# Attention block: the last half's small transfers issued from ScalarE's queue, and a second set of PSUM banks for the output projection

## The chip, the cores and the metric

The kernel runs on one NeuronCore of a Trainium2 chip. The metric is the device time in microseconds (us). It was run three times: 1845.27 us is the median, 1840.76 the lowest and 1845.5 the highest.

## What is computed

The reference is one block with attention and a feed-forward part beside each other. The input is 4 batches of 1024 tokens of width 256. There are 16 heads of 64, taken as 8 pairs. The feed-forward weights and activations are rounded to FP4 in blocks of 16.

```python
xn = _layernorm(x, axis=-1)
x = x + attn(xn, Wq, Wkv, Wout, bout) + ffn(xn, w_gate, w_up, w_down)
# attn: q, k, v = split_heads(xn @ Wq, xn @ Wkv); q, k = _rope(q), _rope(k)
#       sim = einsum('bhid,bhjd->bhij', q, k) * SCALE; p = softmax(sim)
#       out = einsum('bhij,bhjd->bhid', p, v) -> (b, n, 1024);  out @ Wout + bout
```

## The kernel before

The kernel has four parts, written out for each engine: preparation, feed-forward, attention and output. The order of an engine's instructions is the order of the code, and semaphores order the engines among each other. Every DMA is issued by SyncE (sp) from its one queue, in which SyncE also waits: a wait there holds back all transfers behind it.

**Attention** runs in 32 steps s (4 batches times 8 pairs of heads), each of two halves of 512 queries. Halves are numbered 0 to 63. A half's unnormalised output grows in the PSUM bank `o_ps` (bank 7) and is copied to `o_raw` by ScalarE (`copy_o`). Its row sums come from a product with ones in `misc_ps` (bank 2) and are copied to `sum_rows` by ScalarE (`copy_sums`, L1256). Then six transfers and two small operations follow. `store_sums` (L1318) writes the sums to HBM and reads them back in compact form, 8 values to a partition. VectorE takes the reciprocal (`invert`, L1119). `spread_inverse` (L1326) writes that to HBM and reads it back spread over the rows, once for each head. GpSimd multiplies (`normalise`, L1171), and `store_o` (L1336) writes the half to `o_scratch`.

**The output** runs over 8 groups n of 4 tiles of 128 tokens. `load_o(n)` reads 2 MB of `o_scratch` into `o_in[n % 2]`. ScalarE copies each tile's high part (`high`, L1513), VectorE subtracts to get the low part (`split`, L1521), and TensorE multiplies by Wout, 24 matrix multiplications to a tile (`multiply`, L1546). VectorE adds the rest, that is the input, the bias and the feed-forward result (`sums`, L1533). SyncE loads that rest (`load_rest`, L1491) and stores the result (`store`, L1497). All groups write tile t into bank 3 + t, so that tile t of group n waits until `sums` has read tile t of group n - 1 (L1542). `o_hl` and `o_in` have two buffers: `high(n)` waits for the multiplications of group n - 2 and `load_o(n)` for `split(n - 2)`.

**The order around the change.** TensorE multiplies group 0, then the sums of half 63, then groups 1 to 7. ScalarE goes: copy_o(63), high(1), copy_sums(63), high(2), high(3) and so on. VectorE goes: sums(0) and split(1) interleaved, invert(63), then split(2), sums(1), split(3), sums(2), and so on to sums(7). SyncE's end of attention is L1416 to L1428, and then its loop over n from 4 is load_o(n), load_rest(n), store(n - 2). In this order load_o(4) stands behind the whole chain of half 63.

PSUM has 8 banks. In attention banks 0, 1, 5 and 6 hold scores, 3 and 4 the estimates of the maxima, 2 projections and sums, 7 the output.

Of the kernel before, what the change touches and what calls it, by code (L numbers as in the profile page):

```python
# [27 lines left out]
P = 128  # L28
# [807 lines left out]
def attention_part(nc, zones, banks, sem, io, kept, output):  # L836
# [48 lines left out]
    scored, exp_done, pv_done, added = kept["scored"], sem("exp_done"), kept["pv_done"], kept["added"]  # L885
    o_copied, sums_copied = sem("o_copied"), sem("sums_copied")
    sum_stored, compact_in, inv_done, inv_stored = sem("sum_stored"), sem("compact_in"), sem("inv_done"), sem("inv_stored")
    inv_spread = [sem(f"inv_spread{i}") for i in range(2)]
    normed = sem("normed")
    o_stored, rest_stored = kept["o_stored"], kept["rest_stored"]  # L890
    bout_in, rest_in, biased, rest_added = sem("bout_in"), [sem(f"rest_in{i}") for i in range(2)], sem("biased"), sem("rest_added")
# [168 lines left out]
    def vector(dve):  # L1060
# [54 lines left out]
        def invert(half):  # L1115

            dve.wait_ge(compact_in, 16 * (half + 1))
            b = half % 2
            nc.vector.reciprocal(inv_compact[:, b, :, :], compact[:, b, :, :]).then_inc(inv_done, 1)  # L1119
# [42 lines left out]
    def gpsimd(pool):  # L1162
        def normalise(half):

            b = half % 2
            pool.wait_ge(inv_spread[b], 32 * (half // 2 + 1))
            pool.wait_ge(o_copied, half + 1)
# [51 lines left out]
    def scalar(act):  # L1219
# [30 lines left out]
        def copy_sums(half):  # L1250
# [5 lines left out]
            nc.scalar.activation(sum_rows[half % 2][:, :], misc_ps[:, 0:SUMS], ACT.Copy).then_inc(sums_copied, 1)  # L1256

        for chunk in (K1, Q0, Q1):
            high(act, 0, chunk)
        ffn_over(act)  # L1260
        for s in range(-1, STEPS + 1):
            for r in range(ROUNDS):
# [21 lines left out]
                if r == 2 and scoring(s - 1):  # L1284
                    copy_sums(2 * (s - 1) + 1)
                if r == 6 and scoring(s):
                    copy_sums(2 * s)
# [21 lines left out]
    def sync(sp):  # L1309
# [110 lines left out]
        store_o(2 * last)  # L1420
        store_sums(2 * last + 1)
        output["load_rest"](sp, 2)
        output["store"](sp, 0)
        output["load_o"](sp, 3)
        spread_inverse(2 * last + 1)
        store_o(2 * last + 1)
        output["load_rest"](sp, 3)
# [29 lines left out]
def output_part(nc, zones, banks, sem, io, kept):  # L1457
# [6 lines left out]
    o_in = [bound("o_in0", [P, PAIRS, GCOL], F32), free("o_in1", [P, PAIRS, GCOL], F32)]  # L1464
    ps = [banks[:, 3 + t, 0:D] for t in range(GRP)]
    GROUPS = TILES // GRP
# [6 lines left out]
    def load_o(sp, n):  # L1473

        b, u = divmod(n, 2)
        if n >= 2:

            sp.wait_ge(o_low, GRP * (n - 1))
        sp.wait_ge(o_stored[u], 16 * HALVES_OF * (b + 1))
        sp.dma_start(o_in[u][:, :, :], io["o_scratch"][b * PAIRS:(b + 1) * PAIRS, :, u * GCOL:(u + 1) * GCOL]  # L1480
                     .rearrange("s p n -> p s n")).then_inc(o_loaded[u], 16)
# [42 lines left out]
    def sums(dve, n, tiles=range(GRP)):  # L1524
# [6 lines left out]
        for t in tiles:  # L1531
            dve.wait_ge(mult_done, n * GRP + t + 1)
            nc.vector.tensor_tensor(out[u][:, t, :], ps[t], rest[u][:, t, :], ALU.add).then_inc(out_ready, 1)  # L1533

    def multiply(pe, n):
# [3 lines left out]
        for t in range(GRP):  # L1539
            pe.wait_ge(o_low, n * GRP + t + 1)  # L1540
            if n:
                pe.wait_ge(out_ready, (n - 1) * GRP + t + 1)  # L1542
            k = 0
            for os, ws in PARTS:
                for c in range(PAIRS):
                    ins = nc.tensor.matmul(ps[t], o_hl[n % 2][:, os, c, t * P:(t + 1) * P],  # L1546
                                           wo[:, ws, c * D:(c + 1) * D], start=k == 0, stop=k == 3 * PAIRS - 1)
# [34 lines left out]
def build(nc, io):  # L1582
    with ExitStack() as whole:
# [18 lines left out]
        for name in ("x_low", "silu_done", "h_done", "h_high", "down_done", "res_ready", "wo_low", "misc_done", "turn_done", "scored",  # L1602
                     "pv_done", "added"):
            kept[name] = sem(name)
# [107 lines left out]
```

## Time and profile before

| | us |
|---|---|
| median of three runs | 1845.27 |
| lowest and highest | 1840.76 and 1845.5 |
| the profiled execution | 1844.23 |
| its span | 1842.5 |
| TensorE busy | 1760.6 (96%) |
| VectorE busy | 1448.3 (79%) |
| ScalarE busy | 1064.8 (58%) |
| GpSimd busy | 1396.5 (76%) |

The profile is of one execution. Its span runs from the first to the last instruction, and 1.7 us lie around it. PE is TensorE's multiplication, PEld its loading of weights, DVE VectorE, ACT ScalarE, POOL GpSimd, and SPq the queue of SyncE. A time such as 1761.18 is in us from the start of the span. A bracket behind an instruction says how long its engine stood idle before it and what ended that.

### The profile page before, as it was taken

The numbers are of one execution on the slowest core, as the hardware profiler recorded it, in microseconds if no ns is written. First come the engines' busy times: TensorE is split into PE (matmuls) and PEld (weight loads), VectorE is DVE, ScalarE is ACT, GpSimd is POOL, SyncE is SP. The second block draws the span as 40 slices with busy tenths as digits, with TensorE's granted clock in tenths as the row PEclk, the third lists the DMA queues.
The fourth block names the chain that finished last, engine by engine and source line by source line (L and its number), as shares of the span: only waits on it lengthen the run. The fifth ranks groups of instructions, "written<-read, shape, count | busy, mean of one in ns | idle before, by whom it ended". The sixth has DMA issues, their size and how long they took to land.

```text
span 1842.5 us, 29200 instructions
## 1 busy us (share of the span) xinstructions
PE 1760.6 (96%) x10596; PEld 1088.6 (59%) x10596; DVE 1448.3 (79%) x2034; ACT 1064.8 (58%) x1334; POOL 1396.5 (76%) x688
## 2 busy tenths in 40 slices
PE   6979999968999999999999999999999999999889
PEld 4768999944555555555555555555555555554589
DVE  7978999978788878887888788778877887884353
ACT  4642333315666666666666666666666666667531
POOL 3863544415898989999989899999899999999800
PEclk9999999988999999999999999999999999999899
DMA  8651221121233342332224322333433233322574
GB/s 290 238 201 43 73 105 38 47 72 46 73 86 89 93 139 85 88 89 86 85 90 127 104 85 88 87 86 86 127 94 100 84 90 85 87 73 77 186 264 154
DMA packets 164591, 195.11 MB, mean 106 GB/s; under 512 B 48352, under 2 KB 112736, under 8 KB 164192
## 3 DMA queue, kind: packets, MB, share of 16 engines
q1 hardware_dynamic: 164448, 193.25, 33.5%
q8 instruction: 84, 1.38, 0.3%
q14 instruction: 59, 0.48, 0.1%
HBM read 133.69 MB, written 59.51 MB: 105 GB/s over the span
## 4 chain that ended last, share of the span: by engine, by line
PE 61%; DVE 21%; issue 6%; POOL 2%; DMA 2%; ACT 1%; SPq 0%; DVEq 0%; POOLq 0%; ACTq 0%
PE banks L1025 19%; PE banks L1003 15%; PE banks L945 11%; PE banks L979 8%; PE banks L1546 3%; DVE half_max L1069 3%; PE banks L1008 3%; PE banks L1034 2%; DVE h_scales L110 2%; DVE banks L1103 2%; POOL acc L1189 2%; DMA o_in<-o_scratch 2%; DVE f_y L131 2%; DVE f_amax L109 2%; DVE f_y L134 2%
## 5 line engine op out<-in xcount | busy, mean ns | idle before, releaser
L1189 POOL TENSOR_TENSOR acc<-acc,prob 128x1024 f32<-128x1024 f32 x384 | 919.0, 2393 | 78.9 <-ACT prob L1228 46.7
L1069 DVE TENSOR_REDUCE half_max<-banks 128x2 f32<-128x1024 f32 x512 | 627.2, 1226 | 217.9 <-PE banks L979 215.5
L1228 ACT ACTIVATE prob<-banks 128x1024 f32<-128x1024 f32 x512 | 509.8, 1023 | 397.5 <-PE banks L1008 389.8
L1025 PE MATMUL banks<-prob,v 128*64 128x512 f32 x2048 | 495.7, 605 | 0.0
L1240 ACT ACTIVATE banks<-max_all 128x1024 f32<-128x1024 f32 x256 | 263.4, 1029 | 15.3 <-DVE half_max L1069 3.4
L1025 PEld LDWEIGHTS banks<-prob,v 128*64 128x64 f32 x2048 | 124.4, 136 | 227.6 <-issue 189.9
L979 PE MATMUL banks<-k_hi,q_hi 64*128 64x512 f32 x1024 | 232.1, 451 | 17.8 <-DVE half_max L1069 16.2
L979 PEld LDWEIGHTS banks<-k_hi,q_hi 64*128 64x128 f32 x1024 | 96.5, 186 | 233.5 <-issue 125.9
L1189 POOL TENSOR_TENSOR acc<-prob,prob 128x1024 f32<-128x1024 f32 x64 | 153.8, 2402 | 91.9 <-ACT prob L1228 91.9
L945 PE MATMUL banks<-xT,wqk 128*128 128x512 f32 x768 | 217.3, 419 | 2.1 <-DVE k_lo L1112 2.1
L1003 PE MATMUL banks<-q_hi,k_hi 64*128 64x512 f32 x1024 | 204.3, 395 | 8.7 <-ACT prob L1228 8.7
L1003 PE MATMUL banks<-q_hi,k_lo 64*128 64x512 f32 x1024 | 202.5, 391 | 0.0
L1003 PE MATMUL banks<-q_lo,k_hi 64*128 64x512 f32 x1024 | 202.0, 390 | 0.0
L945 PEld LDWEIGHTS banks<-xT,wqk 128*128 128x128 f32 x768 | 137.4, 192 | 61.3 <-issue 33.5
L135 POOL TENSOR_TENSOR f_y<-f_y,f_m 128x704 f32<-128x704 f32 x32 | 54.7, 1710 | 130.0 <-DVE f_y L134 130.0
L732 PE MATMUL banks<-wgT,xqT 128*128 128x352 f32 x768 | 133.9, 329 | 6.3 <-DVE h L583 4.5
L732 PEld LDWEIGHTS banks<-wgT,xqT 128*128 128x128 f32 x768 | 123.7, 190 | 8.7 <-DVE h L583 6.5
L1092 DVE TENSOR_TENSOR crossed<-banks,rope 128x512 f32<-128x512 f32 x128 | 88.5, 691 | 41.2 <-PE banks L945 39.6
L1003 PEld LDWEIGHTS banks<-q_hi,k_hi 64*128 64x128 f32 x1024 | 97.1, 186 | 26.5 <-ACT prob L1228 12.8
L1003 PEld LDWEIGHTS banks<-q_hi,k_lo 64*128 64x128 f32 x1024 | 96.8, 185 | 22.7
L1003 PEld LDWEIGHTS banks<-q_lo,k_hi 64*128 64x128 f32 x1024 | 96.8, 185 | 22.1
L1546 PE MATMUL banks<-wo,o_hl 128*128 128x256 f32 x768 | 95.8, 288 | 6.9 <-DVE out L1533 6.7
(121 smaller groups left out, 2138.5 us busy)
## 6 DMA issues: line engine op xcount, KB each, us to landing
max_all<-max_scratch SPq DMA_DIRECT2D x64, 512.0 KB, 4.1
v_scratch<-v_out SPq DMA_DIRECT2D x32, 512.0 KB, 2.6
wqk<-wp_scratch SPq DMA_DIRECT2D x32, 512.0 KB, 3.8
v<-v_scratch SPq DMA_DIRECT2D x32, 512.0 KB, 5.9
inv_rows<-inv_scratch SPq DMA_DIRECT2D x128, 128.0 KB, 3.3
o_scratch<-o_norm SPq DMA_DIRECT2D x64, 256.0 KB, 2.2
o_in<-o_scratch SPq DMA_DIRECT2D x8, 2048.0 KB, 11.2
xn_scratch<-p_xT SPq DMA_DIRECT2D x32, 256.0 KB, 2.9
```

The costliest lines, as they stand in the source:

```text
L732: ins = nc.tensor.matmul(ps[:, a, 0:FH], xqT[:, t, xs, c, :], wgT[:, ws, c, w, a * FH:(a + 1) * FH], start=k == 0, stop=k == 3 * DC - 1)
L945: ins = nc.tensor.matmul(bank(s, chunk), wqk[s % 2][:, ws, c, col:col + P], xT[:, 4 * half:4 * half + 4, xs, c, :], start=k == 0, stop=k = ...
L979: ins = nc.tensor.matmul(guess_bank(s, i)[:, head, :], q_hi[s % 3][rows, t * P:(t + 1) * P], k_hi[s % 3][rows, part * 512:(part + 1) * 512 ...
L1003: ins = nc.tensor.matmul(s_ps[n % 2][:, head, :], left[rows, keys], right[rows, queries], start=k == 0 and not has_seed, stop=k == 2 and h ...
L1008: ins = nc.tensor.matmul(s_ps[n % 2][:, head, :], first_row[rows, :], max_all[half][rows, head, :], start=False, stop=True)
L1025: ins = nc.tensor.matmul(o_ps[head * DH:(head + 1) * DH, :], v[s % 2][:, kt, at:at + DH], prob[n % SLOTS][:, head, :], start=kt == 0, stop ...
L1069: nc.vector.tensor_reduce(half_max[:, half % 2, :, t % GRP, part], guess_bank(s, i), axis=AX.X, op=ALU.max, negate=True).then_inc(half_max ...
L1092: nc.vector.tensor_tensor(crossed[a][:, :], bank(s, chunk), rope[:, 1, pos], ALU.mult).then_inc(crossed_done, 1)
L1189: nc.gpsimd.tensor_tensor(acc[b][:, :, :], first, prob[n % SLOTS][:, :, :], ALU.add).then_inc(added, 1)
L1228: nc.scalar.activation(prob[n % SLOTS][:, :, :], s_ps[n % 2][:, :, :], ACT.Exp).then_inc(exp_done, 1)
L1240: nc.scalar.activation(s_ps[n % 2][:, :, :], max_all[u // QT][:, :, :].bitcast(F32), ACT.Copy).then_inc(seeded, 1)
L1546: ins = nc.tensor.matmul(ps[t], o_hl[n % 2][:, os, c, t * P:(t + 1) * P], wo[:, ws, c * D:(c + 1) * D], start=k == 0, stop=k == 3 * PAIRS - 1)
```

## The change

The six transfers of half 63 move from SyncE's queue to ScalarE's. `finish_last_half` is placed in ScalarE's order right behind copy_sums(63), ahead of high(2), with its own semaphores (`end_sums`, `end_compact`, `end_inv`, `end_spread`, `end_o`), for which invert, normalise and load_o(7) wait. They are gone from SyncE's order. Groups of odd number use banks 0, 1, 2 and 7 in place of 3 to 6; tile t of group n waits for the sums of group n - 2, and group 1 for the copies out of banks 2 and 7.

```diff
@@ -883,10 +883,11 @@
     max_turn = sem("max_turn")
     max_stored, max_in = [sem(f"max_stored{i}") for i in range(2)], [sem(f"max_in{i}") for i in range(2)]
     scored, exp_done, pv_done, added = kept["scored"], sem("exp_done"), kept["pv_done"], kept["added"]
-    o_copied, sums_copied = sem("o_copied"), sem("sums_copied")
+    o_copied, sums_copied = kept["o_copied"], kept["sums_copied"]
     sum_stored, compact_in, inv_done, inv_stored = sem("sum_stored"), sem("compact_in"), sem("inv_done"), sem("inv_stored")
     inv_spread = [sem(f"inv_spread{i}") for i in range(2)]
     normed = sem("normed")
+    end_sums, end_compact, end_inv, end_spread = sem("end_sums"), sem("end_compact"), sem("end_inv"), sem("end_spread")
     o_stored, rest_stored = kept["o_stored"], kept["rest_stored"]
     bout_in, rest_in, biased, rest_added = sem("bout_in"), [sem(f"rest_in{i}") for i in range(2)], sem("biased"), sem("rest_added")
 
...
@@ -1114,7 +1115,10 @@
 
         def invert(half):
 
-            dve.wait_ge(compact_in, 16 * (half + 1))
+            if half == HALVES - 1:
+                dve.wait_ge(end_compact, 16)
+            else:
+                dve.wait_ge(compact_in, 16 * (half + 1))
             b = half % 2
             nc.vector.reciprocal(inv_compact[:, b, :, :], compact[:, b, :, :]).then_inc(inv_done, 1)
 
...
@@ -1163,7 +1167,10 @@
         def normalise(half):
 
             b = half % 2
-            pool.wait_ge(inv_spread[b], 32 * (half // 2 + 1))
+            if half == HALVES - 1:
+                pool.wait_ge(end_spread, 32)
+            else:
+                pool.wait_ge(inv_spread[b], 32 * (half // 2 + 1))
             pool.wait_ge(o_copied, half + 1)
             if half >= 2:
 
...
@@ -1254,6 +1261,23 @@
 
                 act.wait_ge(sum_stored, 16 * (half - 1))
             nc.scalar.activation(sum_rows[half % 2][:, :], misc_ps[:, 0:SUMS], ACT.Copy).then_inc(sums_copied, 1)
+
+        def finish_last_half():
+
+            half = HALVES - 1
+            b = half % 2
+            act.wait_ge(sums_copied, half + 1)
+            act.dma_start(io["sum_scratch"][b].rearrange("h (k c) -> (h k) c", k=2), sum_rows[b][0:P:QROWS, :]).then_inc(end_sums, 16)
+            act.wait_ge(end_sums, 16)
+            act.dma_start(compact[:, b, :, :], io["sum_scratch"][b].rearrange("h (p f) -> p h f", f=GRP)).then_inc(end_compact, 16)
+            act.wait_ge(inv_done, half + 1)
+            act.dma_start(io["inv_scratch"][b].rearrange("h (p f) -> p h f", f=GRP), inv_compact[:, b, :, :]).then_inc(end_inv, 16)
+            act.wait_ge(end_inv, 16)
+            for head in range(2):
+                act.dma_start(inv_rows[b][head * DH:(head + 1) * DH, :],
+                              io["inv_scratch"][b, head].partition_broadcast(DH)).then_inc(end_spread, 16)
+            act.wait_ge(normed, half + 1)
+            act.dma_start(io["o_scratch"][half // 2, :, b * GCOL:(b + 1) * GCOL], o_norm[b][:, :]).then_inc(kept["end_o"], 16)
 
         for chunk in (K1, Q0, Q1):
             high(act, 0, chunk)
...
@@ -1283,6 +1307,8 @@
                     copy_o(2 * s)
                 if r == 2 and scoring(s - 1):
                     copy_sums(2 * (s - 1) + 1)
+                if r == 2 and s == STEPS:
+                    finish_last_half()
                 if r == 6 and scoring(s):
                     copy_sums(2 * s)
 
...
@@ -1418,12 +1444,9 @@
         spread_inverse(2 * last)
         output["load_o"](sp, 2)
         store_o(2 * last)
-        store_sums(2 * last + 1)
         output["load_rest"](sp, 2)
         output["store"](sp, 0)
         output["load_o"](sp, 3)
-        spread_inverse(2 * last + 1)
-        store_o(2 * last + 1)
         output["load_rest"](sp, 3)
         output["store"](sp, 1)
 
...
@@ -1462,7 +1485,7 @@
     rest = [left(f"rest{i}", [P, GRP, D], F32) for i in range(2)]
     out = [left(f"out{i}", [P, GRP, D], F32) for i in range(2)]
     o_in = [bound("o_in0", [P, PAIRS, GCOL], F32), free("o_in1", [P, PAIRS, GCOL], F32)]
-    ps = [banks[:, 3 + t, 0:D] for t in range(GRP)]
+    ps = [[banks[:, k, 0:D] for k in group] for group in ((3, 4, 5, 6), (0, 1, 2, 7))]
     GROUPS = TILES // GRP
     HALVES_OF = PAIRS
 
...
@@ -1476,7 +1499,11 @@
         if n >= 2:
 
             sp.wait_ge(o_low, GRP * (n - 1))
-        sp.wait_ge(o_stored[u], 16 * HALVES_OF * (b + 1))
+        if n == GROUPS - 1:
+            sp.wait_ge(o_stored[u], 16 * (HALVES_OF * (b + 1) - 1))
+            sp.wait_ge(kept["end_o"], 16)
+        else:
+            sp.wait_ge(o_stored[u], 16 * HALVES_OF * (b + 1))
         sp.dma_start(o_in[u][:, :, :], io["o_scratch"][b * PAIRS:(b + 1) * PAIRS, :, u * GCOL:(u + 1) * GCOL]
                      .rearrange("s p n -> p s n")).then_inc(o_loaded[u], 16)
 
...
@@ -1530,7 +1557,7 @@
             dve.wait_ge(stored[u], 16 * (n // 2))
         for t in tiles:
             dve.wait_ge(mult_done, n * GRP + t + 1)
-            nc.vector.tensor_tensor(out[u][:, t, :], ps[t], rest[u][:, t, :], ALU.add).then_inc(out_ready, 1)
+            nc.vector.tensor_tensor(out[u][:, t, :], ps[u][t], rest[u][:, t, :], ALU.add).then_inc(out_ready, 1)
 
     def multiply(pe, n):
 
...
@@ -1538,12 +1565,16 @@
             pe.wait_ge(kept["wo_low"], 2)
         for t in range(GRP):
             pe.wait_ge(o_low, n * GRP + t + 1)
-            if n:
-                pe.wait_ge(out_ready, (n - 1) * GRP + t + 1)
+            if n >= 2:
+                pe.wait_ge(out_ready, (n - 2) * GRP + t + 1)
+            elif n == 1 and t == 2:
+                pe.wait_ge(kept["sums_copied"], HALVES)
+            elif n == 1 and t == 3:
+                pe.wait_ge(kept["o_copied"], HALVES)
             k = 0
             for os, ws in PARTS:
                 for c in range(PAIRS):
-                    ins = nc.tensor.matmul(ps[t], o_hl[n % 2][:, os, c, t * P:(t + 1) * P],
+                    ins = nc.tensor.matmul(ps[n % 2][t], o_hl[n % 2][:, os, c, t * P:(t + 1) * P],
                                            wo[:, ws, c * D:(c + 1) * D], start=k == 0, stop=k == 3 * PAIRS - 1)
                     k += 1
             ins.then_inc(mult_done, 1)
```

## Rows read from the trace of the kernel before

**Rows 1.** The page, part 1: busy us (share of the span) xinstructions

```profile
PE 1760.6 (96%) x10596; PEld 1088.6 (59%) x10596; DVE 1448.3 (79%) x2034; ACT 1064.8 (58%) x1334; POOL 1396.5 (76%) x688
```

**Rows 2.** Timeline of PE: start us, us, engine, line, operation, out<-in, xcount [idle before]

```profile
1747.72 11.77 PE L1546 MATMUL banks<-wo,o_hl 128*128 128x256 f32 x96
1761.18 23.63 PE L1546 MATMUL banks<-wo,o_hl 128*128 128x256 f32 x192 [1.69 <-DVE out L1533]
1789.86 48.72 PE L1546 MATMUL banks<-wo,o_hl 128*128 128x256 f32 x384 [5.05 <-DVE out L1533]
```

**Rows 3.** Stretches: from:to us, length, busy of engines, PEclk, DMA share, GB/s

```profile
1788.00:1789.00 1.00, 0.00 (x0) 0.00 (x0) 1.00 (x2) 0.00 (x0) 0.00 (x0) 0.76 1.05 387
1795.00:1796.00 1.00, 1.00 (x9) 1.00 (x9) 1.00 (x2) 0.68 (x1) 0.00 (x0) 0.83 1.06 380
```

**Rows 4.** Waits, 1740 to the end: us in total, times, longest

```profile
PE banks L1546 <- DVE out L1533: 6.7, 2, 5.0
```

**Rows 5.** Timelines of ACT and DVE, 1748 to 1792

```profile
1748.80 0.36 ACT L1256 ACTIVATE sum_rows<-banks 128x256 f32<-128x256 f32 x1
1753.47 3.90 ACT L1513 ACTIVATE o_hl<-o_in 128x1024 fp32r<-128x1024 f32 x4 [4.30 <-DMA o_in<-o_scratch]
1783.65 3.90 ACT L1513 ACTIVATE o_hl<-o_in 128x1024 fp32r<-128x1024 f32 x4 [13.98 <-DMA o_in<-o_scratch]
1791.78 3.90 ACT L1513 ACTIVATE o_hl<-o_in 128x1024 fp32r<-128x1024 f32 x4 [4.23 <-DMA o_in<-o_scratch]
...
1784.74 4.63 DVE L1521 TENSOR_TENSOR o_hl<-o_in,o_hl 128x1024 fp32r<-128x1024 f32 x4 [10.84 <-ACT o_hl L1513]
1789.30 1.41 DVE L1533 TENSOR_TENSOR out<-banks,rest 128x256 f32<-128x256 f32 x4
```

**Rows 6.** Timeline of SyncE's queue, 1744 to 1780 (some rows left out)

```profile
1744.25 0.53 SPq L1480 DMA_DIRECT2D o_in<-o_scratch  x1
...
1749.19 0.52 SPq L1322 DMA_DIRECT2D sum_scratch<-sum_rows  x1
1754.32 0.35 SPq L1324 DMA_DIRECT2D compact<-sum_scratch  x1
...
1755.84 0.45 SPq L1480 DMA_DIRECT2D o_in<-o_scratch  x1
1756.33 1.78 SPq L1330 DMA_DIRECT2D inv_scratch<-inv_compact  x1
1765.94 1.10 SPq L1333 DMA_DIRECT2D inv_rows<-inv_scratch  x2
1771.53 0.34 SPq L1340 DMA_DIRECT2D o_scratch<-o_norm  x1
...
1773.06 0.46 SPq L1480 DMA_DIRECT2D o_in<-o_scratch  x1
...
1776.99 3.12 SPq L1480 DMA_DIRECT2D o_in<-o_scratch  x1
```

**Rows 7.** Timelines of SyncE's queue and of POOL: the chain's steps at quieter places

```profile
1611.88 0.53 SPq L1322 DMA_DIRECT2D sum_scratch<-sum_rows  x1
1613.52 0.36 SPq L1324 DMA_DIRECT2D compact<-sum_scratch  x1
...
1740.85 0.45 SPq L1330 DMA_DIRECT2D inv_scratch<-inv_compact  x1
1743.05 1.11 SPq L1333 DMA_DIRECT2D inv_rows<-inv_scratch  x2
...
1746.63 1.83 POOL L1171 TENSOR_TENSOR o_norm<-o_raw,inv_rows 128x512 f32<-128x512 f32 x1 [1.75 <-DMA inv_rows<-inv_scratch]
1770.12 1.38 POOL L1171 TENSOR_TENSOR o_norm<-o_raw,inv_rows 128x512 f32<-128x512 f32 x1 [21.66 <-DMA inv_rows<-inv_scratch]
```

**Rows 8.** Stretches, columns as in rows 3: one with the DMA engines full

```profile
1760.00:1763.00 3.00, 1.81 (x15) 1.85 (x16) 2.03 (x5) 0.00 (x0) 0.00 (x0) 1.00 1.05 404
```

**Rows 9.** Tile compact, its 64 loads: us from issue to landing

```profile
DMA to landing us min/median/max: 1.7/1.7/3.2
```

More of the change, by code:

```diff
@@ L1602, in build @@
         for name in ("x_low", "silu_done", "h_done", "h_high", "down_done", "res_ready", "wo_low", "misc_done", "turn_done", "scored",
-                     "pv_done", "added"):
+                     "pv_done", "added", "end_o", "o_copied", "sums_copied"):
             kept[name] = sem(name)
```

## Prediction

> **What bounds the kernel now.** I read the page first, then only the end of the span, since the diff leaves the instruction order of everything before the last step alone. The busy lines [rows 1] say that TensorE is the bound overall (96%), so the change can only give back idle time of TensorE in the output stage, and it can only cost by making new idle time there. The timeline of TensorE in that stage [rows 2] is to be read for its holes. From group 1 on it runs 96, 192 and 384 multiplications with two holes: 1759.49 (1747.72 + 11.77) to 1761.18, and 1784.81 to 1789.86. That is 1.69 and 5.05 us. A group lasts 11.8 us (23.63 / 2). The last four took 48.72 us where four times 11.77 is 47.08, so 1.64 us more. The stretches of the clock [rows 3] show why: TensorE stopped at 1784.81, the granted clock was down to its lower level (1.2 GHz) by 1789 (mean 0.76 over 1788 to 1789, so it fell about 3.9 us after the stop), and it was back at 2.4 GHz only in the slice 1795 to 1796. After the hole of 1.69 us it did not fall. All that can be won is thus 1.69 + 5.05 + 1.64 = 8.4 us, or 0.45% of the time.
>
> The waits [rows 4] name VectorE's addition L1533 as what ended both holes. The reason lies in the order on VectorE: split(2) and only then sums(1), split(4) and only then sums(3), while the next group needs the bank that sums frees. For the second hole there is more behind it: ScalarE's high(4) started at 1783.65, the moment o_in(4) landed [rows 5], and that load had been issued only at 1773.06, because SyncE's queue stood from 1756.33 to 1771.53 in the chain of the last half (inverse to scratch, spread, normalise, store) [rows 6].
>
> **The change part by part.**
>
> **The second set of banks.** Group n no longer waits for sums(n - 1), but for sums(n - 2), which is over long before. Banks 0, 1, 2 and 7 are free for group 1: the sums are copied out at 1749.16 [rows 5] while tile 2 of group 1 comes at about 1747.72 + 5.9 = 1753.6; o_ps was copied earlier still. No instruction is added but waits that are already met, so the cost is nothing; if the copy came after 1753.6, each us late would be a us of hole. The gain by itself: a group may start when its first split is done. From the start h of high, the split begins 1.1 us later (1783.65 to 1784.74), takes 1.16 us (4.63 / 4), and TensorE follows 0.2 us behind (VectorE's addition ended at about 1789.65, TensorE began at 1789.86): h + 2.5. For group 4 that is 1786.15 where it was 1789.86. With nothing else changed group 2 would start at 1759.5 and the hole before group 4 would be about 1786.15 - 1783.1 = 3.0 us. By then the clock was still at 2.4 GHz in the hole of before. So this part alone is worth 8.4 - 3.0 = 5.4 us.
>
> **The chain off SyncE's queue.** SyncE issued the six transfers of the last half (sum_scratch, compact, inv_scratch, two inv_rows, o_scratch) between its own. Without them load_o(3) goes when split(1) is done, at 1751.9 instead of 1755.84, and load_rest(3), store(1) and load_o(4) are bound by VectorE alone (sums(1), and split(2) for load_o(4)). The last load needs the new end_o, which is over some 30 us before: nothing.
>
> **The chain on ScalarE's queue.** This adds the wait that decides. finish_last_half stands ahead of high(2), and in it ScalarE waits in turn for sum_scratch, for VectorE's reciprocal, for inv_scratch and for GpSimd's normalise. Queued behind it are the four copies high(2) for which split(2) on VectorE waits, behind those sums(1), and so group 2 on TensorE, load_rest(3), store(1) and load_o(4) on SyncE. Before, high(2) ran at 1753.47, as soon as o_in(2) was there. Now it starts at h, when the chain has ended. Undisturbed, by its steps [rows 7]: sum_scratch to the issue of compact 1.64 (1611.88 to 1613.52); compact, reciprocal and issue of inv_scratch 2.01 (1754.32 to 1756.33); inv_scratch 2.20 (1740.85 to 1743.05); the two inv_rows to the start of the normalisation 3.58 (1743.05 to 1746.63); the normalisation and the issue behind it 1.41 (1770.12 to 1771.53); that issue itself 0.34. Sum 11.2, so h is 1749.16 + 11.2 = 1760.4 at the earliest. The time TensorE stands still before group 2 is h + 2.5 - 1759.5, so at least 3.4 us where it was 1.69.
>
> But the chain does not run undisturbed. SyncE's load_o(2) is under way from 1744.25, and behind it now stand load_rest(2) and store(0) (0.5 MB each, about 1749) and load_o(3) (2 MB, at 1751.9): some 5.5 MB with store_o(62), which at the 404 GB/s of a full stretch [rows 8] keep the DMA engines full from about 1746 to 1759.6. No row of this case shows a transfer of a second queue beside a full one. The bounds are these. Below: no delay, h = 1760.4. Above: each waits for all that was issued before it, as on the one queue of before, where sum_scratch took 5.13 us (1749.19 to 1754.32) and inv_scratch 9.61 us (1756.33 to 1765.94). Then compact lands with load_o(3) at about 1760.4, and with 0.3 + 2.20 + 3.58 + 1.41 + 0.34 behind it h is 1768.2; at the very worst the chain keeps its whole length of before, from 1749.16 to 1771.87, and h is 1771.9. I take a value nearer to the lower end: queues that take turns. At 404 GB/s over 16 engines a piece of 2 KB takes 81 ns; compact and inv_scratch are cut in 256 pieces of 16 bytes, 16 to an engine, and if each stands behind one of 2 KB that is 1.3 us for either. sum_scratch has four pieces and the two inv_rows fall behind the full stretch: about 0.1. That is an estimate from these rows: h = 1760.4 + 2.7 = 1763.1.
>
> The Trainium skill, on its page DMA: Bandwidth & Descriptors (Queues, rings and completion order), says that each DMA engine takes turns between the queues that have work for it, a packet at a time, and the section Issuing engines are not separate DMA queues that all of them still run on the same 16 engines. No run here shows either yet. The first speaks for an h between 1760.4 and 1763.1, the second against an undisturbed chain.
>
> **The sum.** After group 2 starts, nothing else is late. load_o(4) is issued after split(2), sums(1), load_rest(3) and store(1), at about h + 8.3; group 4 is due at h + 2.5 + 23.6 = h + 26.1. Even if the load took the 14.8 us that load_o(5) took beside another (1776.99 to 1791.78) it gives a start of h + 8.3 + 14.8 + 2.5 = h + 25.6, just in time; with the 10.6 us of load_o(4) itself there are 4.7 us to spare. The loads behind it keep the rhythm that they had, and there TensorE had no hole. So groups 2 to 7 take 23.63 + 47.08 = 70.7 us, and TensorE ends at h + 2.5 + 70.7, plus the clock. Before it was 1789.86 + 48.72 = 1838.58; what lies behind (one addition, one store) stays. The difference is h - 1765.4, plus 1.64 for the clock where the hole outlasts the 3.9 us after which it fell before, which it does from h = 1760.9 on. With h = 1763.1 the hole is 6.1 us and the difference -2.3 + 1.64 = -0.7 us: the span goes from 1842.5 to 1841.8, the profiled execution from 1844.23 to 1843.5. The median of the three runs (1845.27) lies 1.0 above the profiled one, and I forecast from it: 1844.6.
>
> **The rivals.**
>
> **The chain as quick as undisturbed.** The small transfers pass between the large ones at no price: h = 1760.4, hole 3.4 us, no fall of the clock: -5.0, so 1840.3. For it: they are tiny, and their median landing over 64 halves is short (compact 1.7 us [rows 9]). Against it: every step of the chain but the last lies in the full stretch.
>
> **The small ones wait for the large ones: slower.** A queue of its own does not help, because the pieces of SyncE's loads are already handed to the same engines, or because both queues' pieces are made out by one unit; SyncE's own issue of inv_scratch took 1.78 us right behind load_o(3) against 0.45 for the half before, and load_o(5) 3.12 against 0.46. The place is compact and inv_scratch; the price is h = 1768.2, +2.8 + 1.64 = +4.4, so 1849.7, and up to h = 1771.9, +8.1, so 1853.4. It decides from h = 1763.8 on, where the gain of the banks is used up (h - 1765.4 + 1.64 = 0). Against it: load_o(3) goes 4 us earlier than before, so that it is through when inv_rows are due.
>
> **A second hole remains.** The hole before group 4 stays, because load_o(4) takes longer than any did: 1 us of hole for each us over 15. That speaks only for a little more than the forecast, 1846 to 1848.
>
> **The banks alone count.** If ScalarE's chain hid wholly behind group 1, that is h at most 1757.0, the whole 8.4 us would come back: 1836.9. It would need a chain of 7.8 us, 3.4 less than its undisturbed steps; I see no row for it.
>
> **How the numbers follow.** Forecast (h from 1761.2 to 1766, 1842.7 to 1847.5) 0.5; undisturbed chain (1838.5 to 1842) 0.22; small behind large (1848 to 1853.4) 0.2; second hole 0.06; all comes back 0.02. A measurement of this kernel can tell about 0.3% from no change, that is 5.5 us: under 1839.7 or over 1850.8. Faster takes under half of the undisturbed case and the last: 0.1. Slower takes about half of the third: 0.1. The rest, 0.8, is within. The range of 1839.5 to 1850 leaves out the upper half of the third case and a tail of the second, some 0.15 to 0.2.
>
> **What would show it.** In the profile after: TensorE's timeline of L1546 with one hole, of about 6 us, before group 2, ended by VectorE's split L1521 and no longer by L1533, the low clock behind it, and no hole before group 4; high(2) on ScalarE at 1763 where it was 1753; GpSimd's last normalisation near 1761.5 instead of 1770.12; load_o(4) at about 1771. The landings of compact and inv_scratch under ScalarE's queue settle the rivals: 1.7 and 2.2 us, 3.0 and 3.5, or over 5. It is wrong if the hole before group 2 is under 3 or over 9 us, if a hole shows later, or if anything ahead of 1740 differs.

## The result and the profile after

The change makes the kernel slower, by 0.3%: the median is 1849.85 us (1847.46 to 1850.47, 7 runs) against 1844.05 for the kernel before (1840.76 to 1845.5, 7 runs). The ratio is 1.003, with a 95% interval of 1.0021 to 1.0039. The profiled execution took 1848.66 us with a span of 1846.9, where before it was 1844.23 and 1842.5. Two executions among the experiments' (2860.54 us of chain_only, 3419.98 of late_chain) were in a far slower state; the ratios leave them out, and the medians of these two kernels hardly move by them (0.2 us at most).

The timeline of TensorE after, beside [rows 2]:

```profile
1748.39 11.77 PE L1577 MATMUL banks<-wo,o_hl 128*128 128x256 f32 x96
1771.55 71.39 PE L1577 MATMUL banks<-wo,o_hl 128*128 128x256 f32 x576 [11.39 <-DVE o_hl L1548]
```

Two holes, of 1.69 and 5.05 us, have become one of 11.39. Groups 2 to 7 then run without another, and what ends the hole is no longer the addition but the split. It is the start of everything for group 2 that is late. Of the 4.4 us between the two spans, 0.7 lie ahead of group 1 (1748.39 against 1747.72), where the code is the same; over all the profiled executions of this document group 1 starts between 1746.74 and 1749.29, a spread that no edit here explains. The timelines of ScalarE and its queue, and of VectorE and GpSimd, show what came first (columns as in [rows 2]):

```profile
1748.95 0.36 ACT L1263 ACTIVATE sum_rows<-banks 128x256 f32<-128x256 f32 x1
1749.34 1.08 ACTq L1270 DMA_DIRECT2D sum_scratch<-sum_rows  x1
1754.85 0.39 ACTq L1272 DMA_DIRECT2D compact<-sum_scratch  x1
1761.65 0.37 ACTq L1274 DMA_DIRECT2D inv_scratch<-inv_compact  x1
1763.78 1.14 ACTq L1277 DMA_DIRECT2D inv_rows<-inv_scratch  x2
1768.73 0.34 ACTq L1280 DMA_DIRECT2D o_scratch<-o_norm  x1
1769.18 7.69 ACT L1540 ACTIVATE o_hl<-o_in 128x1024 fp32r<-128x1024 f32 x8 [19.87 <-POOL o_norm L1178]
...
1761.41 0.20 DVE L1123 RECIPROCAL inv_compact<-compact 128x8 f32<-128x8 f32 x1 [9.45 <-DMA compact<-sum_scratch]
1770.27 4.63 DVE L1548 TENSOR_TENSOR o_hl<-o_in,o_hl 128x1024 fp32r<-128x1024 f32 x4 [8.65 <-ACT o_hl L1540]
...
1767.44 1.26 POOL L1178 TENSOR_TENSOR o_norm<-o_raw,inv_rows 128x512 f32<-128x512 f32 x1 [18.83 <-DMA inv_rows<-inv_scratch]
```

ScalarE issues sum_scratch at 1749.34 and comes to high(2) at 1769.18, where it was 1753.47 [rows 5]. From one to the other are 19.84 us. On SyncE's queue in the kernel before, the chain took 22.7 us (1749.19 to 1771.87), but there nothing of group 2 stood behind it. The steps compare with the quiet ones of [rows 7] like this: sum_scratch 5.51 us against 1.64, compact with the reciprocal 6.80 against 2.01, inv_scratch 2.13 against 2.20, inv_rows 3.66 against 3.58. So two steps are long, the two that ran while SyncE's loads were under way, and they are 8.7 us too long together (3.9 for sum_scratch, 4.8 for compact). What SyncE had issued by then:

```profile
1744.55 0.53 SPq L1507 DMA_DIRECT2D o_in<-o_scratch  x1
1748.63 0.34 SPq L1366 DMA_DIRECT2D o_scratch<-o_norm  x1
1749.08 0.40 SPq L1518 DMA_DIRECT2D rest<-rest_scratch  x1
1749.53 0.73 SPq L1524 DMA_DIRECT2D out<-out  x1
1751.99 0.36 SPq L1507 DMA_DIRECT2D o_in<-o_scratch  x1
1776.25 0.36 SPq L1518 DMA_DIRECT2D rest<-rest_scratch  x1
```

The last two rows also show the second cost: behind load_o(3) SyncE issues nothing for 24 us, since load_rest(3) waits for sums(1), and sums(1) stands behind split(2) on VectorE. The profile's DMA answer for two stretches of the changed kernel counts each queue's packets (q1 is SyncE's queue, q10 ScalarE's; packets, MB, share of 16 engines, over 100% where the recorded times of packets overlap). A piece is one such packet of data: compact has 256 of 16 bytes, load_o(3) 1024 of 2 KB. First the stretch that follows the issue of compact, then a microsecond later on:

```profile
q1 hardware_dynamic: 944, 1.31, 105.4%
```

```profile
q1 hardware_dynamic: 186, 0.38, 98.4%
q10 hardware_dynamic: 178, 0.00, 10.1%
```

From 1754.85 to 1758.2 no packet of ScalarE's queue moves at all, though compact has been issued and waits for no semaphore. Its first piece moves at 1758.5, 3.6 us after the issue, and its last at 1760.9. From 1759 to 1760 the two queues move one for one. For inv_scratch, which is cut the same way and ran when only the end of load_o(3) was left, the first piece moved 0.9 us after the issue, and all of them took 0.7 us. So compact landed 4.4 us later than inv_scratch (6.5 us against 2.1), and 2.7 of these are more wait in front of its first piece and 1.7 are taking turns. For sum_scratch the wait was longer: its first piece moved at 1754.0, 4.7 us after its issue.

### The profile page after: what moved, and what is told of

The parts are those of the page before. It is cut to its first block, busy times and chain, and to the rows that moved or that the text cites. A ratio compares the mean times of both kernels' runs of the same rounds, so it can differ in the third digit from the quotient of the medians.

```text
span 1846.9 us, 29198 instructions
## 1 busy us (share of the span) xinstructions
PE 1761.7 (95%) x10596; PEld 1090.2 (59%) x10596; DVE 1446.6 (78%) x2034; ACT 1064.7 (58%) x1334; POOL 1395.4 (76%) x688
## 4 chain that ended last, share of the span: by engine, by line
PE 64%; DVE 20%; issue 6%; POOL 3%; ACT 0%; POOLq 0%; DVEq 0%; ACTq 0%
PE banks L1026 19%; PE banks L1004 16%; PE banks L946 11%; PE banks L980 9%; PE banks L1577 4%; PE banks L1009 3%; DVE half_max L1070 3%; POOL acc L1196 2%; PE banks L1035 2%; DVE h_scales L110 2%; DVE f_y L131 2%; DVE f_amax L109 2%; DVE f_y L134 2%; DVE h L583 1%; DVE banks L1104 1%
```

## The experiments

Changes in time are against the kernel before as run beside each experiment. Its median was 1842.97 us (14 runs) beside banks_only, chain_only, hold_load and late_chain, and 1842.85 (15 runs) beside hold_spread, large_pieces, act_split and pool_chain. Beside the changed kernel itself it was 1844.05, so kernels are compared by their distance from the kernel before: +5.8 us for the changed one. By the intervals of the ratios such a distance is good to 2 or 3 us either way. The diffs show the main lines of each edit; "..." stands for lines left out.

**The two parts by themselves.** `banks_only` is the kernel before with the second set of banks:

```diff
-    ps = [banks[:, 3 + t, 0:D] for t in range(GRP)]
+    ps = [[banks[:, k, 0:D] for k in group] for group in ((3, 4, 5, 6), (0, 1, 2, 7))]
...
-            if n:
-                pe.wait_ge(out_ready, (n - 1) * GRP + t + 1)
+            if n >= 2:
+                pe.wait_ge(out_ready, (n - 2) * GRP + t + 1)
...
```

> The change without its transfers: the second set of banks alone, the chain of half 63 on SyncE's queue as before. Theory (the banks give, the move of the chain takes): group 2 follows group 1 without a hole, high(2) stays near 1753.5, and the hole before group 4 shrinks from 5.05 to about 3.0 us, without the low clock behind it; 5.4 us less than before, about 1838.7. Rival (the loss sits in the new banks, or they give nothing since the loads are what is late): 1844 to 1850, the hole before group 4 still 5 us or more.

Measured: 1839.29 us, ratio 0.9978 (0.9969 to 0.9987), 3.7 us less. TensorE's timeline:

```profile
1748.97 34.81 PE L1550 MATMUL banks<-wo,o_hl 128*128 128x256 f32 x288
1785.91 47.82 PE L1550 MATMUL banks<-wo,o_hl 128*128 128x256 f32 x384 [2.12 <-DVE o_hl L1521]
```

Groups 1 to 3 run in one piece, and before group 4 a hole of 2.12 us is left, ended by the split as the arithmetic wanted. But what was expected of the clock did not come. The row of this kernel for 1787 to 1788 (columns as in [rows 3]) shows TensorE at work with the lower clock:

```profile
1787.00:1788.00 1.00, 1.00 (x7) 1.00 (x6) 1.00 (x1) 0.44 (x1) 0.00 (x0) 0.50 1.07 412
```

The mean granted clock is 0.92 from 1786 to 1787, 0.50 from 1787 to 1790 and 0.88 from 1790 to 1791: it fell near 1786.8, 0.9 us after TensorE had started again. The last four groups took 47.82 us, 1.6 more than four of the 11.56 us that a group takes where nothing stops (late_chain below). The banks are a gain all the same.

`chain_only` is the changed kernel with the old banks and the old wait.

```diff
-    ... for group in ((3, 4, 5, 6), (0, 1, 2, 7))]
+    ... for group in ((3, 4, 5, 6), (3, 4, 5, 6))]
```

> The change without its banks: the chain of half 63 issued by ScalarE, one set of banks. Theory: compact lands over 6 us after its issue as in the changed kernel, high(2) starts at about 1769, and TensorE now waits besides until sums(1) has read the banks, which comes after the whole of split(2), so group 2 starts some 3.5 us later still: about 1853.3. Rival (the move by itself costs little, the two parts only get in each other's way): about 1844 to 1847.

Measured: 1852.26 us, ratio 1.0046 (1.0032 to 1.006), 9.3 us more; compact landed after 6.5 us again, high(2) began at 1768.46, and group 2 in this row:

```profile
1774.66 71.81 PE L1573 MATMUL banks<-wo,o_hl 128*128 128x256 f32 x576 [14.09 <-DVE out L1560]
```

The hole of 14.09 us is ended by the addition again. So the move of the chain costs 9.3 us and the banks give 3.7; the sum of the two, 5.6, is close to the 5.8 of the change, though with 2 or 3 us of doubt in each it is a weak test. With the chain in place the banks bring 9.3 - 5.8 = 3.5 us.

**What makes the chain long.** `hold_load` lets SyncE issue load_o(3) only when inv_scratch has landed:

```diff
+        sp.wait_ge(kept["end_inv"], 16)
         output["load_o"](sp, 3)
```

> The changed kernel with one wait more: SyncE issues load_o(3), the 2 MB load that runs beside the chain, only once inv_scratch has landed. Theory (the small transfers on ScalarE's queue wait for the pieces that SyncE has issued before them): compact lands about 2.5 us after its issue in place of 6.5, inv_scratch keeps its 2.1, high(2) starts near 1765 in place of 1769.2, and the time is 4.1 us under that of the changed kernel, about 1845.8. Rival (transfers issued by ScalarE, or reading back what has just been written, are slow by themselves): compact still 6 us or more, 1849.9 or above since load_o(3) comes later.

Measured: 1850.24 us, ratio 1.0036 (1.0023 to 1.005), +7.3 us and no gain over the changed kernel. The queue of ScalarE shows both why the theory stands and why my number fell:

```profile
1754.10 0.39 ACTq L1272 DMA_DIRECT2D compact<-sum_scratch  x1
1756.89 0.37 ACTq L1274 DMA_DIRECT2D inv_scratch<-inv_compact  x1
1758.50 1.15 ACTq L1277 DMA_DIRECT2D inv_rows<-inv_scratch  x2
1768.30 0.34 ACTq L1280 DMA_DIRECT2D o_scratch<-o_norm  x1
```

compact took 2.79 us to the next issue in place of 6.80. But load_o(3) went at 1758.50, in the same moment as inv_rows, and now inv_rows were slow: they landed 6.5 and 7.9 us after their issue. I had let the load start one step too early, and the wait had only moved to it. `hold_spread` waits for both inv_rows instead:

```diff
+        sp.wait_ge(kept["end_spread"], 32)
         output["load_o"](sp, 3)
```

> As hold_load, but SyncE issues load_o(3) only once both inv_rows have landed, so that no large load is issued while the chain runs. In hold_load the reciprocal came 4.75 us earlier than in the changed kernel, and the two inv_rows, issued at the same moment as load_o(3), took 6.5 and 7.9 us in place of 3. Theory (a small transfer pays for what is issued before or with it, on either queue): inv_rows 3 us again, high(2) at about 1764 in place of 1769, load_o(3) still in time, 4.5 us under the changed kernel, about 1845. Rival (the chain is held by something else, such as ScalarE's own issuing): high(2) still near 1768, about 1850.

Measured: 1844.52 us, ratio 1.0011 (1.0001 to 1.002), +1.7 us, which is 4.1 less than the changed kernel's +5.8. The landings are 3.0 (compact) and 3.2 us (inv_rows). In this execution everything is 0.7 us later than in the one of the changed kernel, and high(2) starts 16.3 us after the copy of the sums where it was 20.2:

```profile
1749.61 0.36 ACT L1263 ACTIVATE sum_rows<-banks 128x256 f32<-128x256 f32 x1
1765.91 3.90 ACT L1541 ACTIVATE o_hl<-o_in 128x1024 fp32r<-128x1024 f32 x4 [15.94 <-POOL o_norm L1178]
...
1768.28 71.80 PE L1578 MATMUL banks<-wo,o_hl 128*128 128x256 f32 x576 [7.22 <-DVE o_hl L1549]
```

So it is load_o(3) beside the chain that made it 3.9 us longer, and not ScalarE's issuing. The 16.3 us still hold 5.6 for sum_scratch, which runs beside load_o(2). No run took load_o(2) away, so that these 5.6 us, too, come from loads under way is argued: from 1.64 us at a quiet place [rows 7], 5.13 on SyncE's queue before and from the packets.

**What a small transfer waits for.** `large_pieces` is the changed kernel in which load_o(3) has 8 pieces to an engine in place of 64. Group 3 is computed from other parts of o_scratch.

```diff
+        if n == 3:
...
+            sp.dma_start(o_in[u][:, :, :].rearrange("p s n -> p (s n)"),
+                         io["o_scratch"][at:at + 4].rearrange("s p n -> (s p n)").rearrange("(q m) -> q m", q=P)) ...
```

> The changed kernel, in which load_o(3) reads the same 2 MB in 128 pieces of 16 KB in place of 1024 pieces of 2 KB; they are other parts of o_scratch, so group 3 is computed from wrong data. It tells apart what compact waits for. In the changed kernel its first piece moved 3.6 us after the issue, behind 984 pieces of SyncE's queue (62 to an engine) or 1.4 MB. If a fixed number of pieces stands ahead: all 8 large pieces of each engine come first, compact lands only when load_o(3) is through, 7.5 us or more after its issue. If a fixed number of bytes: 6.5 us as before. If the making of the pieces is what it waits for: 3 us or less, since there are 8 times fewer, and high(2) starts near 1765.

Measured: compact landed after 9.0 us, and the single time was 1849.84. The number is near that of the first theory, but the packets say something else. From 1754.64 (the issue of compact) to 1758, and from 1758.5 to 1761:

```profile
q1 hardware_dynamic: 865, 1.47, 115.0%
```

```profile
q1 hardware_dynamic: 67, 1.10, 102.4%
q10 hardware_dynamic: 65, 0.00, 1.5%
```

In front of the first piece lies the same wait as in the changed kernel, some 3.5 us and 1.4 MB or a little more; and then the queues take turns by the piece, 65 pieces of 16 bytes against 67 of 16 KB. None of the three answers that I had written down is right by itself. The length has two parts, a wait in front and a turn for each piece, and only the second grew with the pieces of load_o(3).

Two runs ask what the wait in front is. Both start from hold_load, where inv_rows and load_o(3) are issued together while nothing else moves. `hold_large` gives load_o(3) its 128 large pieces as above, and `hold_small` 1024 pieces of 256 bytes:

```diff
+            sp.dma_start(o_in[u][:, :, 0:64], io["o_scratch"][b * PAIRS:(b + 1) * PAIRS, :, u * GCOL:u * GCOL + 64]
...
```

> As hold_load (load_o(3) issued by SyncE at the same moment as inv_rows by ScalarE, nothing else under way), but load_o(3) reads its 2 MB in 128 pieces of 16 KB in place of 1024 of 2 KB, from other parts of o_scratch, so group 3 is computed from wrong data. In hold_load the first piece of inv_rows moved 3.7 us after the issue. If what holds a small transfer back is the making of the pieces of the transfer issued before it, the first piece of inv_rows moves within 1.5 us of the issue here; if it is the bytes under way, after 3 us or more as there. Then the two queues take turns piece by piece, 8 to an engine against pieces of 0.65 us, so that inv_rows lands 6 us or more after its issue in either case.

> As hold_load, but load_o(3) reads only 64 of the 512 columns, 256 bytes a piece: still 1024 pieces, but 0.25 MB; the rest of o_in keeps what load_o(1) left, so group 3 is computed from wrong data. If the making of the pieces holds inv_rows back, its first piece moves 3 us or more after the issue as in hold_load, and it lands after 5 us or more; if the bytes under way do, within 1.5 us, and it lands after about 3.

Measured: single times of 1850.14 us (`hold_large`) and 1847.81 (`hold_small`), where the kernel before took 1842.89 beside them; and, by stretches of the DMA answer, the following. `hold_load`, 1758.5 to 1762.2 (nothing of q10), then 1762.2 to 1763:

```profile
q1 hardware_dynamic: 229, 0.47, 63.9%
```

```profile
q1 hardware_dynamic: 124, 0.25, 82.9%
q10 hardware_dynamic: 28, 0.06, 18.4%
```

`hold_large`, 1758.4 to 1763 (nothing of q10), then 1763 to 1765:

```profile
q1 hardware_dynamic: 63, 1.03, 70.5%
```

```profile
q1 hardware_dynamic: 47, 0.77, 92.5%
q10 hardware_dynamic: 31, 0.06, 8.2%
```

`hold_small`, 1761.2 to 1762.9 (nothing of q10):

```profile
q1 hardware_dynamic: 204, 0.05, 12.9%
```

What the same two transfers do with nothing beside them, `hold_spread` shows: issued at 1760.4, nothing until 1762.0, and from 1762 to 1764 all of both:

```profile
q10 hardware_dynamic: 160, 0.26, 49.2%
```

So with no load at all the first piece of inv_rows moves 1.6 us after the issue. Beside the 2 KB pieces it was 3.9 us (1762.4), beside the 16 KB pieces 5.2 (1763.6), and beside the 256 byte pieces 2.2 (1763.4). What the load adds is 2.3, 3.6 and 0.6 us. The landings were 6.5 and 7.9, 8.9 and 9.3, 4.0 and 4.1 us, against 3.2 alone. Both runs speak for the bytes under way, though `hold_small` missed the numbers written down for that (1.5 us to the first piece, 3 to the landing). The fewest pieces made the longest wait, and 1024 small ones added 0.6 us, so the making of the pieces is at most a small part of it. It goes with the bytes that are under way, but not with a fixed number of them (0.47 MB in one case, 1.03 in the other). Nor are the 16 engines full in that time: q1's share is 63.9% and 70.5%. Where exactly these bytes stand stays open. One for one, too, is shown for compact only: beside inv_rows 124 pieces of q1 moved against 28, and 47 against 31.

**The place of the waits.** `act_split` keeps the chain on ScalarE's queue, beside the same loads, and only puts its steps behind ScalarE's own work; VectorE's reciprocal goes behind sums(1):

```diff
                 high(act, n, t)
+            if n == 2:
+                output["compact_back"]()
+            if n == 3:
+                output["inverse_to_o"]()
```

> The changed kernel with ScalarE's part of the chain cut up: sum_scratch is issued where it was, compact behind high(2), the inverse and all behind it after high(3), and VectorE's reciprocal after sums(1). The chain stays on ScalarE's own queue, with the same loads beside it. Theory (the loss is the place of the waits, not the queue): no hole before group 2; high(4) waits until the chain is over, near 1781, which is before o_in(4) is needed: 1835.7 or up to 2 us more if a hole is left before group 4. Rival (ScalarE's issuing or its queue costs by itself): 1842 or more.

Measured: 1836.14 us, ratio 0.9961 (0.9948 to 0.9973). compact landed after 6.6 us and inv_scratch after 6.3, longer than in the changed kernel, the chain ended at 1773.8, and TensorE has no hole at all in the profiled execution, which was the fastest of five (1833.37 us; the others took 2 to 4 us more, and what they lost is in no trace):

```profile
1746.74 80.89 PE L1588 MATMUL banks<-wo,o_hl 128*128 128x256 f32 x672
```

From +5.8 to -6.7 us is a gain of 12.5, with small transfers as slow as before. Only the place of the waits has changed, on ScalarE and, for the reciprocal, on VectorE.

`pool_chain` lets GpSimd issue the chain, with the reciprocal in the same place as in act_split.

> The chain issued by GpSimd, which has nothing else to do by then, with the new banks and VectorE's reciprocal after sums(1). Nothing waits behind it but GpSimd's last normalisation. Theory: no hole from group 1 to 7, about 1835, though the chain itself is as long as on the other queues (compact over 5 us to landing) since the loads run beside it. Rival (a queue apart from the hardware's escapes the large loads): the same time, but compact lands in 3 us or less. If GpSimd's issuing disturbs the other engines: 1838 or more.

Measured: 1834.15 us, ratio 0.9953 (0.9938 to 0.9969). The small transfers were hardly quicker on GpSimd's queue (rows of its timeline):

```profile
1748.13 0.74 POOL L1186 DMA_DIRECT2D sum_scratch<-sum_rows  x1 [1.01 <-ACT sum_rows L1285]
1754.23 0.77 POOL L1188 DMA_DIRECT2D compact<-sum_scratch  x1 [5.37 <-DMA sum_scratch<-sum_rows]
...
1768.02 1.08 POOL L1193 DMA_DIRECT2D inv_rows<-inv_scratch  x2 [6.99 <-DMA inv_scratch<-inv_compact]
```

5.37 and 6.99 us of waiting for 4 KB each; compact landed after 5.5. The DMA answer, from 1754.3 to 1758 (nothing of q0, which is GpSimd's queue), then from 1758 to 1760:

```profile
q1 hardware_dynamic: 789, 1.47, 103.9%
```

```profile
q1 hardware_dynamic: 337, 0.67, 95.1%
q0 software_dynamic: 32, 0.00, 2.2%
```

The wait in front is here too, 3.8 us or more. A queue apart does not escape the loads. That compact landed a microsecond sooner than on ScalarE's queue may come from its cut, 32 packets in place of 272 and so fewer turns; no run here separates the two.

`late_chain` leaves the chain on SyncE's queue and puts its steps where SyncE would wait anyway; the three entries of "end" issue inv_scratch, the two inv_rows and o_scratch. The reciprocal goes behind sums(1) as in act_split:

```diff
-        store_sums(2 * last + 1)
+        sums_out(2 * last + 1)
         output["load_rest"](sp, 2)
         output["store"](sp, 0)
         output["load_o"](sp, 3)
-        spread_inverse(2 * last + 1)
-        store_o(2 * last + 1)
+        sums_back(2 * last + 1)
...
             load_o(sp, n)
+            if n == 4:
+                output["end"][0]()
             load_rest(sp, n)
+            if n == 4:
+                output["end"][1]()
             store(sp, n - 2)
+            if n == 4:
+                output["end"][2]()
```

> The new banks, and the chain of half 63 kept on SyncE's queue but out of the way: its steps stand behind load_o(3), load_o(4) and load_rest(4) wherever SyncE would wait anyway, and VectorE's reciprocal comes after sums(1) in place of before split(2). Only load_o(7) needs the half, near 1800. Theory (all 8.4 us lie in the order of the queues): no hole on TensorE from group 1 to group 7, 1835.7. Rival (load_o(4), now issued near 1762, is held back by the small transfers or by the other loads, and the hole before group 4 stays at 3 us): 1838.7.

Measured: 1834.12 us, ratio 0.9949 (0.9936 to 0.9963). compact landed only after 9.6 us, and it did not matter. The timelines of SyncE's queue and of TensorE:

```profile
1752.43 1.40 SPq L1333 DMA_DIRECT2D compact<-sum_scratch  x1
...
1761.02 0.45 SPq L1499 DMA_DIRECT2D o_in<-o_scratch  x1
1762.27 1.93 SPq L1345 DMA_DIRECT2D inv_scratch<-inv_compact  x1
1773.32 1.11 SPq L1352 DMA_DIRECT2D inv_rows<-inv_scratch  x2
...
1747.17 80.89 PE L1569 MATMUL banks<-wo,o_hl 128*128 128x256 f32 x672
```

load_o(4) goes at 1761.02 in place of 1773.06 [rows 6], and all seven groups run in one piece. This is as fast as with GpSimd's queue, with no second queue, and faster than both kernels: 8.9 us under the one before.

## Why the prediction was wrong

The forecast was 1844.6 us, 0.7 less than before; what came was 5.8 more. That 1849.85 still lies inside the range of 1839.5 to 1850 is no merit of the working.

**What bounds the kernel:** right. Apart from the 0.7 us ahead of group 1 the difference lies in the output stage, and the two holes with the clock were what could be won. Their size was put a little low. In one piece seven groups take 80.89 us, so one takes 11.56 and not 11.8; from the start of group 1 to the end of group 7 it was 90.86 before (1747.72 to 1838.58). So 10.0 us could be won, not 8.4. In that account the low clock after the hole of before cost 48.72 - 4 x 11.56 = 2.5 us and not 1.64. In the medians of late_chain 8.9 us came back, with an interval of 6.8 to 11.8.

**The banks:** the gain was right in kind, and so was the place and the end of the hole that stayed (2.12 us where 3.0 were forecast). 3.7 us were measured where 5.4 were worked out, and 5.4 is within the interval (2.4 to 5.7). What failed is the clock. The prediction let it fall only in a hole that outlasts 3.9 us, by the one fall of before, and so gave the banks the whole 1.64 us back. In banks_only it fell after a hole of 2.12 us and took 1.6, which is about what 3.7 lacks of 5.4. The rows give no fixed delay: from the stop to the fall it was 3.7 us before (0.76 over 1788 to 1789 puts the fall at 1788.5, not 3.9 us after the stop), 3.1 in banks_only with TensorE already at work, and 2.4 in the changed kernel (stop at 1760.16, mean 0.76 over 1762 to 1763). After the hole of 1.69 us of before it did not fall.

**The wait on ScalarE's queue:** right in kind. What stands behind it was named (high(2), split(2), sums(1), load_rest(3), load_o(4)), the hole is where it was to be, ended by the split, and no other came behind it. h + 2.5 was h + 2.4. For h = 1769.18 the formula h - 1765.4 + 1.64 gives 5.4 us, where the spans differ by 4.4: its groups of 11.8 us are too long.

**The step that failed is the price of the chain beside the loads.** I had h = 1763.1, from 2.7 us of delay over the undisturbed chain; it was 1769.18, 8.8 us over it. By terms: sum_scratch was given 0.1 us with inv_rows, and alone cost 3.9 (5.51 against 1.64); compact was given 1.3 and cost 4.8 (6.80 against 2.01); inv_scratch was given 1.3 and cost nothing (2.13 against 2.20), because load_o(3) was nearly through. The 1.3 us for taking turns piece by piece was sound for compact (178 packets against 186 in a microsecond, and 1.7 us by its first and last piece). What was missing is the wait in front of the first piece: 3.6 us for compact where a like transfer in a quiet stretch waits 0.9, and 4.7 us for sum_scratch. No turn-taking explains it. What exactly a transfer waits for there stays open. I gave sum_scratch next to no delay, since it has only four pieces; but a wait in front does not ask how many pieces follow. The row that warned was my own upper bound, the 5.13 us that sum_scratch took before [rows 6]: it took 5.51 on ScalarE's queue. I discounted it because it was measured on one queue, and chose the lower end with nothing measured in its favour.

The Trainium skill's rule on taking turns (DMA: Bandwidth & Descriptors, Queues, rings and completion order) agrees with the traces once both queues' pieces move: 65 against 67 packets, even where one side's are a thousand times larger. That section of the Trainium skill has an engine stay with one queue for a whole packet, typically of about 9 to 17 descriptors; here the turn was a single piece, and the traces decide. Its other section, Issuing engines are not separate DMA queues, agrees too: beside the loads compact landed after 9.6 us on SyncE's queue (late_chain), 6.5 on ScalarE's and 5.5 on GpSimd's (cut in fewer packets there), against 1.7 when quiet. Read as a price, as I did, the first rule leaves out the wait in front.

**The rivals.** The third, small behind large, came nearest: its h was 1768.2 (1769.18 measured) and its change of the time +4.4 us (+5.8 by the medians, +4.4 by the profiled executions). It had only 0.2 of the chance. That 1849.7 and 1849.85 agree so well is luck in part, since the median of before was 1845.27 then and 1844.05 beside the result. Its place was half right: it named compact and inv_scratch, and it was sum_scratch and compact. Its cause was half right too: compact landed at 1761.4 where 1760.4 was worked out, but not behind all of load_o(3), which landed at 1763.6; and the making of the pieces is at most a small part of it. The rival with a second hole and the one with an undisturbed chain fell: only inv_scratch and inv_rows had their quiet length, and they ran when the loads were through. That the banks alone might count was rightly given little for this kernel: the whole gain came (8.9 us in late_chain), but only with the chain behind the urgent work.

## What to carry to other kernels

A queue of its own spares an engine the wait of another queue's order, but here its transfers shared the 16 DMA engines with the loads of the other queue. Price a small transfer beside large ones by the slowest landing that a trace has for such a stretch, not by its quiet landing. A chain of dependent transfers whose result is needed late belongs behind the work that is needed soon: ask of each engine what stands behind the wait, and put each step where that engine would wait anyway. Here, with the same banks and the same queue, the place alone made the difference between +5.8 and -6.7 us; with the steps so placed, ScalarE's, GpSimd's and SyncE's queue gave -6.7, -8.7 and -8.9, and the intervals of the three overlap.

## What the runs showed of the hardware

A small transfer issued behind or together with a large one on another queue waits before its first piece moves: 3.6 us for compact and 4.7 for sum_scratch in the changed kernel, against 0.9 for inv_scratch in a quiet stretch. For inv_rows it was 1.6 us alone, 3.9 beside 2 MB in pieces of 2 KB, 5.2 in pieces of 16 KB, and 2.2 beside 0.25 MB in pieces of 256 bytes. Then the queues alternated piece by piece for compact, beside pieces of 2 KB (178 against 186) and of 16 KB (65 against 67), so that large pieces on one queue slow the other: compact landed after 6.5 us beside pieces of 2 KB, 9.0 beside pieces of 16 KB, and 1.7 when quiet. The wait in front was there on ScalarE's and on GpSimd's queue alike.

The granted clock of TensorE fell to its lower level after holes of 2.12 us (banks_only), 5.05 (before) and 11.39 (changed), and did not after one of 1.69 (before). The loss behind them was 1.6, 2.5 and 2.0 us, by groups of 11.56.
